# Deformable convolution on one core: spread matmuls of three groups interleaved part by part, and a chunk's twelfth group run with the next chunk's first two

## The chip, the core and the metric

The kernel runs on one core of a Trainium2 chip. The metric is device microseconds of one whole execution. TensorE is called PE here, VectorE DVE, ScalarE ACT, GpSimd POOL and SyncE SP. What an engine's own instruction reader does (register steps, branches, waits of their own) is listed in the profile under the engine's name with a q, as PEq or PEldq.

## What is computed

The input is 8 images of 32 channels, 64x64 pixels. It is normalised per channel and image, passes four blocks and one final deformable convolution, and is added to the raw input:

```python
def _block(x, dc_w, dc_b, of_w, of_b, dw, db):
    h = jax.nn.relu(_deconv2d(x, dc_w, dc_b))          # 3x3, 32 -> 32 channels
    offset = _conv2d(h, of_w, of_b, PAD)               # 3x3, 32 -> 18: (dy, dx) of 9 taps
    return jax.nn.relu(_deform_conv2d(h, offset, dw, db))
...
sampled = bilinear samples of x at (row + tap + dy, column + tap + dx), zero outside
out = einsum('bckhw,ock->bohw', sampled, w) + b
...
x_cat = concatenate(x, in_module)                      # 64 channels
offset = _conv2d(x_cat, fin_off_w, fin_off_b, PAD)
return _deform_conv2d(x_cat, offset, fin_dcn_w, fin_dcn_b)
```

## The kernel before

The images go in two sets of four. A step is one layer for one set, so there are ten: eight of the four blocks, two of the final layer. A step begins with 3x3 convolutions on PE (line 515), then picks by the range of the offsets how wide a window of pixels the samples can come from. In this data the eight block steps take `kind` 0 (window 11x11, 121 positions) and the two final steps `kind` 1 (16x16, in two tiles of 128).

The sampling takes nearly all of a step. The image plane is cut into 32 chunks (16 bands of four rows, two halves). A bilinear weight is a product of a hat function in y and one in x, and the hats are made once for a chunk: ACT takes the distance (`DIST`, line 735), DVE clamps it (line 922), POOL casts it to fp16 and makes the rest as a second fp16 part (`HL`, lines 1103 and 1105, semaphore `hats_full`). The hats sit on four blocks of 32 partitions, one for each image. A *group* is three taps of one image; a chunk has twelve (a kind 1 chunk has two batches of twelve), and group g lies on the 32 partitions of image g mod 4. For a group:

- PE spreads the y hats over the window's positions with a 0/1 table `SEL`: two matmuls, one for each part of `HL` (line 544), into one of three y slots of PSUM; the second raises `y_full`. In this text they are the first and second part of y.
- ACT copies that slot to SBUF (`YC`, line 768), which raises `y_ready`.
- PE spreads the x hats the same way, into one of four x slots (two matmuls, or four for the two tiles of kind 1; `x_full`).
- DVE multiplies the two (`A`, line 917, `product_done`).

A y spread waits until the copy three groups earlier is done, an x spread until the product four groups earlier is done. Both waits are written with a register value, so PE's reader does a register step ahead of each group.

When a chunk's twelve products are there, PE samples: matmuls of `A` with the window's pixels `VT` (line 562) in three parts, each of which ACT copies out of the one PSUM bank `PS` (`SMP`, line 745). Then comes the sum over taps and channels (`deform`, line 575), which ACT takes out (`TMP`, line 728) and DVE adds to the image (line 911). A part of the chunk before runs after groups 4, 7 and 10 of the present one (`sh.after`), the sum of an earlier chunk after group 1 (`sum_after`; in kind 1 only in the second batch).

All of this is one order written out by hand for each engine; semaphores alone tie them together. The chunk loop is unrolled by two: chunks 0 and 1, a hardware loop over pairs, chunks 30 and 31. So every second chunk border is a loop's branch (line 297), the other runs straight through. On ACT the order at a border is: third part's `SMP`, `YC` of group 11, `DIST` of the chunk after the one that begins, `YC` of groups 0 and 1, `TMP`. PE waits at the head of a chunk's body for the chunk's hats (line 630, which the trace shows as line 253), and POOL's order has nothing but the hats.

In kind 0 PE issues y and x of one group, then y and x of the next (lines 613 to 615). In kind 1 it issues the y spreads of a run of groups and then their x spreads (lines 616 to 621); the runs are groups 0-1, 2-4, 5-7, 8-10 and 11.

Of the kernel before, what the change touches and what calls it, by code (L numbers as in the profile page):

```python
# [22 lines left out]
BLK = 4  # L23
COLS = 32
CPX = BLK * COLS
BANDS = SIDE // BLK
CHUNKS = 2 * BANDS
# [73 lines left out]


# [7 lines left out]
def build(nc, t):  # L110

    ctx = ExitStack()
    with ctx:
# [388 lines left out]
        def _(pe):  # L502
# [31 lines left out]
            def spread(sh, g, b, par, table, out, column=0):  # L534

                third, i = divmod(g, IMG)
                q = slice(CH * i, CH * (i + 1))
                for part in range(2):
                    hats = HL[q, part, par, 3 * CPX * third:3 * CPX * (third + 1)]
                    dst = P[0:sh.npos, out, column:column + sh.size]  # L540
                    if sh.kind == 1:
                        hats = hats.rearrange("p (k r c) -> p k r c", r=BLK, c=COLS)[:, :, :, 16 * b:16 * b + 16]
                        dst = dst.rearrange("p (k r c) -> p k r c", r=BLK, c=16)
                    mm = nc.tensor.matmul(dst, SEL[q, table, 0:sh.npos], hats, start=part == 0, stop=part == 1)  # L544
                return mm
# [33 lines left out]
            def body_of(sh):  # L579
# [19 lines left out]
                def batch(c, b, half, prev, before):  # L599
                    def spread_y(g):  # L600

                        pe.wait_ge(y_ready, (c * sh.batches + b) * sh.ngr + g + 1)
                        spread(sh, g, b, half, y_table, g % Y_SLOTS).then_inc(y_full, 1)

                    def spread_x(g):

                        pe.wait_ge(product_done, (c * sh.batches + b) * sh.ngr + g + 1)
                        for tile, table in enumerate(x_tables):
                            mm = spread(sh, g, b, half, table, Y_SLOTS + g % X_SLOTS, sh.size * tile)
                        mm.then_inc(x_full, 1)  # L610

                    for g in range(sh.ngr):
                        if sh.kind == 0:
                            spread_y(g)
                            spread_x(g)
                        elif g in sh.runs:

                            for each in sh.runs[g]:
                                spread_y(each)
                            for each in sh.runs[g]:  # L620
                                spread_x(each)
# [597 lines left out]
```

## Time and profile before

| | |
|---|---|
| time, median of 3 runs | 4313.63 us (4312.2 to 4316.89) |
| the profiled execution: span | 4314.1 us (the page gives no other time of it) |
| PE busy, weight loads | 3880.1 us (90%), 2973.5 us (69%) |
| DVE busy | 2952.5 us (68%) |
| ACT busy | 2786.4 us (65%) |
| POOL busy | 1140.5 us (26%) |
| spread matmuls, line 544 | 21504, 1745.6 us busy |
| copies of y, line 768 | 4608, 1733.9 us busy |
| products, line 917 | 4608, 2311.4 us busy |

The time of the profiled execution lies within the three timed runs, 0.5 us above their median, and nothing is shown outside its span. Busy time of PE is the union of matmuls that overlap: a matmul that is listed with 0.32 us can run beside others. A row of the timeline merges instructions of one kind that follow each other; its first two numbers are the start and the length in us.

### The profile page before, as it was taken

The page shows a single profiled execution, that of the slowest core. Times are in us where ns is not written, and L with a number is a line of the kernel's source. Part 1 is how long each engine was busy: PE and PEld are TensorE (multiplying, and loading weights), DVE is VectorE, ACT ScalarE, POOL GpSimd, SP SyncE. Part 2 cuts the span into 40 slices and gives each one's busy share as a digit, 9 for nine tenths or more (in the row PEclk, how much of TensorE's full clock was granted, in tenths as well). Part 3 has the DMA queues.
Part 4 walks back from the last instruction along what each step waited for, and adds up shares of the span by engine and source line. Part 5 has one row for each costly group of instructions (what it writes and reads, how often), then busy time and mean ns, then how long its engine had stood idle before and what let it go on. Part 6 is the DMA issues. An engine that isn't in the chain of part 4 may idle for free.

```text
span 4314.1 us, 221726 instructions
## 1 busy us (share of the span) xinstructions
PE 3880.1 (90%) x81908; PEld 2973.5 (69%) x81908; DVE 2952.5 (68%) x5858; ACT 2786.4 (65%) x6651; POOL 1140.5 (26%) x645
## 2 busy tenths in 40 slices
PE   4998799699789879979988997998799999799998
PEld 3776577477567657756765775776577777577776
DVE  5885687488567668847856884784577774577775
ACT  2885588388478658837865883885355554255554
POOL 0441243134033214403322431331111110111111
PEclk8999899799989989989998997999799999899999
DMA  4442544344244334424424443443766664666664
GB/s 125 127 127 66 143 125 110 89 126 127 75 132 126 90 106 127 125 76 131 126 71 127 127 114 92 126 125 109 179 154 152 150 150 127 147 154 152 152 150 110
DMA packets 244838, 533.50 MB, mean 124 GB/s; under 512 B 61200, under 2 KB 151824, under 8 KB 227216
## 3 DMA queue, kind: packets, MB, share of 16 engines
q1 hardware_dynamic: 194224, 498.67, 45.0%
q10 hardware_dynamic: 50240, 29.89, 2.4%
q8 instruction: 229, 3.75, 0.4%
q14 instruction: 145, 1.19, 0.1%
HBM read 471.87 MB, written 56.45 MB: 122 GB/s over the span
## 4 chain that ended last, share of the span: by engine, by line
PE 68%; SPq 18%; issue 7%; ACT 2%; DMA 2%; DVE 2%; POOLq 0%; ACTq 0%; DVEq 0%; POOL 0%; PEld 0%; PEldq 0%
PE P L544 26%; PE PS L562 24%; SPq L380 9%; PE P L515 8%; PE PS L575 8%; SPq L388 8%; SPq L370 1%; PE PS L515 1%; ACT H L848 1%; DMA X<-x_dram 1%; PE P L530 1%; DVE FOFF L1032 1%; DMA VT<-ht_store 0%; DVE A L917 0%; DVE ST L1036 0%
## 5 line engine op out<-in xcount | busy, mean ns | idle before, releaser
L917 DVE TENSOR_TENSOR A<-P,YC 121x384 f32<-121x384 f32 (+1 forms) x4608 | 2311.4, 550 | 850.1 <-ACT YC L768 684.5
L544 PE MATMUL P<-HL,SEL 32*121 32x384 f16 (+1 forms) x21504 | 1745.6, 304 | 131.6 <-issue 95.3
L768 ACT ACTIVATE YC<-P 121x384 f32<-121x384 f32 (+1 forms) x4608 | 1733.9, 444 | 98.7 <-PE P L544 65.8
L544 PEld LDWEIGHTS P<-HL,SEL 32*121 32x121 f16 (+1 forms) x21504 | 1126.9, 117 | 513.9 <-issue 228.6
L562 PE MATMUL PS<-A,VT 121*32 121x80 f32 (+1 forms) x40960 | 1342.7, 250 | 51.7 <-DMA VT<-ht_store 15.5
L562 PEld LDWEIGHTS PS<-A,VT 121*32 121x32 f32 (+1 forms) x40960 | 1093.0, 117 | 354.6 <-issue 200.4
L1103 POOL CAST HL<-DIST 128x1152 f16<-128x1152 f32 x320 | 366.3, 1145 | 3066.1 <-DVE DIST L922 3043.8
L745 ACT ACTIVATE SMP<-PS 128x480 f32<-128x480 f32 (+3 forms) x1152 | 593.9, 516 | 638.2 <-PE PS L562 632.9
L1105 POOL TENSOR_TENSOR HL<-DIST,HL 128x1152 f16<-128x1152 f32 x320 | 769.6, 2405 | 58.5 <-POOL HL L1103 58.5
L735 ACT ACTIVATE DIST<-HB,CONST 128x1152 f32<-128x1152 f32 x320 | 400.8, 1252 | 231.4 <-DMA HB<-off_store 128.8
L575 PE MATMUL PS<-SMP,CW 128*64 128x128 f32 x7424 | 476.0, 277 | 5.4 <-ACT SMP L745 5.4
L575 PEld LDWEIGHTS PS<-SMP,CW 128*64 128x64 f32 x7424 | 398.7, 137 | 86.8 <-issue 76.6
L515 PE MATMUL P<-X,W 32*32 32x512 f32 x5040 | 210.0, 664 | 90.7 <-POOLq L256 58.6
L922 DVE TENSOR_SCALAR DIST<-DIST 128x1152 f32<-128x1152 f32 x320 | 240.2, 751 | 10.2 <-ACT DIST L735 10.2
L911 DVE SCALAR_TENSOR_TENSOR X<-X,CONST,TMP 128x128 f32 (+1 forms) x320 | 172.5, 539 | 79.7 <-ACT TMP L728 79.7
L515 PEld LDWEIGHTS P<-X,W 32*32 32x32 f32 x5040 | 128.4, 108 | 141.5 <-issue 114.6
L728 ACT ACTIVATE TMP<-PS,BIAS 128x128 f32<-128x128 f32 x320 | 119.0, 372 | 151.5 <-PE PS L575 151.5
L848 ACT ACTIVATE H<-P,BIAS 32x512 f32<-32x512 f32 x128 | 87.9, 687 | 193.6 <-PE P L515 161.6
L515 PE MATMUL P<-H,W 32*32 32x512 f32 x5040 | 209.5, 637 | 2.7 <-issue 2.7
L1032 DVE SCALAR_TENSOR_TENSOR FOFF<-P,PXB 128x512 f32<-128x512 f32 x70 | 47.9, 684 | 198.5 <-PE PS L515 122.3
L515 PEld LDWEIGHTS P<-H,W 32*32 32x32 f32 x5040 | 138.4, 105 | 62.6 <-issue 29.5
L1016 DVE TENSOR_SCALAR H<-P,BIAS 32x512 f32<-32x512 f32 x96 | 72.0, 750 | 145.8 <-PE P L515 118.3
(61 smaller groups left out, 703.4 us busy)
## 6 DMA issues: line engine op xcount, KB each, us to landing
HB<-off_store SPq DMA_DIRECT2D x2560, 72.0 KB
VT<-ht_store SPq DMA_DIRECT2D x256, 512.0 KB
VT<-ht_store SPq DMA_DIRECT2D x768, 132.0 KB
VT<-ht_store SPq DMA_DIRECT2D x256, 88.0 KB
off_store<-FOFF SPq DMA_DIRECT2D x160, 128.0 KB, 2.6
H<-x_dram SPq DMA_DIRECT2D x5, 2048.0 KB, 14.6
ht_store<-A ACTq DMA_DIRECT2D x32, 256.0 KB, 3.3
ht_store<-VT ACTq DMA_DIRECT2D x32, 256.0 KB, 3.9
```

Of the source, the lines that this page charges most:

```text
L380: sp.dma_start(HB[q:q + AXIS, half, :], src).then_inc(hb_full[half], 16)
L388: sp.dma_start(VT[first:first + sh.win * columns, buf, tile * size:(tile + 1) * size], src).then_inc(vt_full[buf], 16)
L515: mm = nc.tensor.matmul(bank(bank0 + i)[CH * j:CH * (j + 1), :], weights[q, CH * k:CH * (k + 1)], view(row + k // 3 - 1, col + k % 3 - 1)[ ...
L544: mm = nc.tensor.matmul(dst, SEL[q, table, 0:sh.npos], hats, start=part == 0, stop=part == 1)
L562: mm = nc.tensor.matmul(PS[q:q + wide, sh.unit * v:sh.unit * (v + 1)].rearrange("p (k y x) -> p k y x", k=sh.taps, y=BLK), vt[:, img, :], ...
L575: mm = nc.tensor.matmul(PS[64 * pair:64 * (pair + 1), 0:CPX], CW[:, 64 * k:64 * (k + 1)], rhs, start=k == 0, stop=k == sh.taps - 1)
L735: nc.scalar.activation(DIST[:, :], HB[:, half, :], ACT.Abs, bias=HAT_BIAS).then_inc(abs_done, 1)
L745: nc.scalar.activation(smp_px(0, sh, b * sh.blocks + w, s, count), PS[:, 0:sh.unit * count], ACT.Copy).then_inc(ps_free, 1)
L768: nc.scalar.activation(YC[0:sh.npos, g % X_SLOTS, 0:sh.size], P[0:sh.npos, g % Y_SLOTS, 0:sh.size], ACT.Copy).then_inc(y_ready, 1)
L917: return nc.vector.tensor_tensor(dst, x, y, ALU.mult)
L1103: nc.gpsimd.tensor_copy(HL[:, 0, half, :], DIST[:, :]).then_inc(hat_step, 1)
L1105: nc.gpsimd.tensor_tensor(HL[:, 1, half, :], DIST[:, :], HL[:, 0, half, :], ALU.subtract).then_inc(hats_full, 1)
```

## The change

PE's order of spread matmuls is written anew; no other engine's code is touched. A run takes up to three groups, of either kind: the first parts of their y, the second parts, then the first parts of their x, the second parts (in kind 1 for one tile and then the other). Where no sample part stands after group 11, which is so in both kinds here, group 11 (`carries`) is left out of its own chunk or batch and put in front of the next one's run of groups 0 and 1. At a chunk border that place is behind the loop's branch and behind the wait for the new chunk's hats. After the last chunk, group 11 runs alone.

```diff
+        self.carries = int(self.ngr - 1 not in self.after)
...
-            def spread(sh, g, b, par, table, out, column=0):
+            def spread_part(sh, g, b, par, table, out, column, part):
...
+                return nc.tensor.matmul(dst, SEL[q, table, 0:sh.npos], hats, start=part == 0, stop=part == 1)
...
-                    for g in range(sh.ngr):
-                        if sh.kind == 0:
-                            spread_y(g)
-                            spread_x(g)
-                        elif g in sh.runs:
-
-                            for each in sh.runs[g]:
-                                spread_y(each)
-                            for each in sh.runs[g]:
-                                spread_x(each)
+                def run(members):
+
+                    if len(members) > Y_SLOTS:
+                        run(members[:Y_SLOTS])
+                        members = members[Y_SLOTS:]
+                    for n, g, b, half in members:
+                        pe.wait_ge(y_ready, n + 1)
+                        spread_part(sh, g, b, half, y_table, g % Y_SLOTS, 0, 0)
+                    for n, g, b, half in members:
+                        spread_part(sh, g, b, half, y_table, g % Y_SLOTS, 0, 1).then_inc(y_full, 1)
+                    for tile, table in enumerate(x_tables):
+                        for part in range(2):
+                            for n, g, b, half in members:
+                                if tile == 0 and part == 0:
+                                    pe.wait_ge(product_done, n + 1)
+                                mm = spread_part(sh, g, b, half, table, Y_SLOTS + g % X_SLOTS, sh.size * tile, part)
+                                if tile == len(x_tables) - 1 and part == 1:
+                                    mm.then_inc(x_full, 1)
+
+                def batch(c, b, half, prev, before, carried):
+                    first = (c * sh.batches + b) * sh.ngr
+                    for g in range(sh.ngr - sh.carries):
+                        if g in sh.runs:
+                            members = [(first + each, each, b, half) for each in sh.runs[g]]
+                            if sh.runs[g][0] == 0 and sh.carries and carried is not None:
+                                members.insert(0, (first - 1, sh.ngr - 1, *carried))
+                            run(members)
...
                 def tail():
+                    if sh.carries:
+                        run([(CHUNKS * sh.batches * sh.ngr - 1, sh.ngr - 1, sh.batches - 1, 1)])
```

PE at the border in the middle of a loop's pair of chunks, kind 0: before, the third part (line 562) is followed by group 11's four spreads, and only then by the wait for the hats and group 0.

```order
L562 MATMUL PS<-A,VT 32x80 x15
L602 REGISTER_ALU
L544 MATMUL P<-HL,SEL 121x384 [waits y_ready]
L544 MATMUL P<-HL,SEL 121x384
L544 MATMUL P<-HL,SEL 121x384 [waits product_done]
L544 MATMUL P<-HL,SEL 121x384
L252 REGISTER_ALU
L602 ISA [waits hats_full]
L544 MATMUL P<-HL,SEL 121x384 [waits y_ready]
L544 MATMUL P<-HL,SEL 121x384
```

The same place in the change, whose lines 545, 567 and 610 are the old 544, 562 and 602: group 11's first spread is the first one below the wait for the hats.

```order
L567 MATMUL PS<-A,VT 32x80 x15
L254 REGISTER_ALU
L610 REGISTER_ALU [waits hats_full]
L545 MATMUL P<-HL,SEL 121x384 [waits y_ready]
L610 REGISTER_ALU
L545 MATMUL P<-HL,SEL 121x384 [waits y_ready]
L610 REGISTER_ALU
L545 MATMUL P<-HL,SEL 121x384 [waits y_ready]
L545 MATMUL P<-HL,SEL 121x384 x3
L545 MATMUL P<-HL,SEL 121x384 [waits product_done] x3
L545 MATMUL P<-HL,SEL 121x384 x3
```

Group 11 moved behind the wait, and the second part of its y moved behind two more register steps and the first parts of groups 0 and 1.

PE at the end of the loop's body, kind 0: before, group 11 stands between the third part and the branch.

```order
L562 MATMUL PS<-A,VT 32x80 x15
L602 REGISTER_ALU
L544 MATMUL P<-HL,SEL 121x384 [waits y_ready]
L544 MATMUL P<-HL,SEL 121x384
L544 MATMUL P<-HL,SEL 121x384 [waits product_done]
L544 MATMUL P<-HL,SEL 121x384
L297 REGISTER_ALU
L297 COMPARE_AND_BRANCH
```

In the change the branch follows the third part at once, and group 11 is found at the head of the loop's body.

```order
L545 MATMUL P<-HL,SEL 121x384 x3
L596 REGISTER_ALU [waits product_done]
L567 MATMUL PS<-A,VT 32x80 [waits ps_free]
L567 MATMUL PS<-A,VT 32x80 x15
L299 REGISTER_ALU
L299 COMPARE_AND_BRANCH
```

PE between the two batches of a kind 1 chunk: before, all six spreads of group 11 stand ahead of groups 0 and 1 (the sum, line 596, follows).

```order
L562 MATMUL PS<-A,VT 64x144 x7
L602 REGISTER_ALU
L544 MATMUL P<-HL,SEL 128x192 [waits y_ready]
L544 MATMUL P<-HL,SEL 128x192
L544 MATMUL P<-HL,SEL 128x192 [waits product_done]
L544 MATMUL P<-HL,SEL 128x192 x3
L602 ISA
L544 MATMUL P<-HL,SEL 128x192 [waits y_ready]
L544 MATMUL P<-HL,SEL 128x192
L602 REGISTER_ALU
```

In the change the three groups go in step.

```order
L567 MATMUL PS<-A,VT 64x144 x7
L610 ISA
L545 MATMUL P<-HL,SEL 128x192 [waits y_ready]
L610 REGISTER_ALU
L545 MATMUL P<-HL,SEL 128x192 [waits y_ready]
L610 REGISTER_ALU
L545 MATMUL P<-HL,SEL 128x192 [waits y_ready]
L545 MATMUL P<-HL,SEL 128x192 x3
L545 MATMUL P<-HL,SEL 128x192 [waits product_done] x3
L545 MATMUL P<-HL,SEL 128x192 x9
```

Here no wait for hats and no branch lies between; group 0 and 1 moved up beside group 11.

## Rows read from the trace of the kernel before

**Rows 1.** The page, chain that ended last, by line

```profile
PE P L544 26%; PE PS L562 24%; SPq L380 9%; PE P L515 8%; PE PS L575 8%; SPq L388 8%; SPq L370 1%; PE PS L515 1%; ACT H L848 1%; DMA X<-x_dram 1%; PE P L530 1%; DVE FOFF L1032 1%; DMA VT<-ht_store 0%; DVE A L917 0%; DVE ST L1036 0%
```

**Rows 2.** Timeline of ACT over two chunks of the first step (start, us, instructions)

```profile
207.48 1.26 ACT L735 ACTIVATE DIST<-HB,CONST 128x1152 f32<-128x1152 f32 x1
208.64 0.85 ACT L768 ACTIVATE YC<-P 121x384 f32<-121x384 f32 x2
...
213.48 0.57 ACT L745 ACTIVATE SMP<-PS 128x480 f32<-128x480 f32 x1 [0.31 <-PE PS L562]
213.95 1.25 ACT L768 ACTIVATE YC<-P 121x384 f32<-121x384 f32 x3
215.13 0.44 ACT L745 ACTIVATE SMP<-PS 128x320 f32<-128x320 f32 x1
215.56 0.49 ACT L768 ACTIVATE YC<-P 121x384 f32<-121x384 f32 x1
215.95 1.25 ACT L735 ACTIVATE DIST<-HB,CONST 128x1152 f32<-128x1152 f32 x1
```

**Rows 3.** Groups by line and shape: kind 0 copies of y (busy, mean, idle before)

```profile
L768 ACT ACTIVATE YC<-P 121x384 f32<-121x384 f32 x3072 | 1319.9, 500 | 18.7 <-PE P L544 17.0
```

**Rows 4.** Timeline of DVE, same chunk

```profile
209.24 1.02 DVE L917 TENSOR_TENSOR A<-P,YC 121x384 f32<-121x384 f32 x2 [1.31 <-ACT YC L768]
210.18 0.75 DVE L922 TENSOR_SCALAR DIST<-DIST 128x1152 f32<-128x1152 f32 x1
...
212.31 1.94 DVE L917 TENSOR_TENSOR A<-P,YC 121x384 f32<-121x384 f32 x4
```

**Rows 5.** Busy time of DVE from its first product of that chunk (window, us, busy, clock)

```profile
209.24:214.25 5.01, 5.01 (x10) 1.00 0.36 103
```

**Rows 6.** Timeline of PE, same chunk

```profile
211.30 1.14 PE L544 MATMUL P<-HL,SEL 32*121 32x384 f16 x12
...
213.35 1.02 PE L544 MATMUL P<-HL,SEL 32*121 32x384 f16 x12
214.30 0.76 PE L562 MATMUL PS<-A,VT 121*32 121x80 f32 x32
```

**Rows 7.** Timeline of POOL, same chunk

```profile
212.42 2.41 POOL L1105 TENSOR_TENSOR HL<-DIST,HL 128x1152 f16<-128x1152 f32 x1 [0.18 <-POOL HL L1103]
```

**Rows 8.** Single steps of PE's reader, each asked for alone (length ns, start)

```profile
L602 PEldq ALU_OP  x1: 32/32/32, 205.8 to 205.8; - x1
L297 PEldq ALU_OP  x1: 32/32/32, 205.9 to 205.9; - x1
...
L253 PEldq EVENT_SEMAPHORE  x1: 51/51/51, 214.9 to 214.9; - x1
L602 PEldq FUSED_REGOPS  x1: 37/37/37, 215.0 to 215.0; - x1
L602 PEldq ALU_OP  x1: 32/32/32, 215.1 to 215.1; - x1
```

**Rows 9.** Timeline of PE at 206.28, 206.66, 206.667 and 215.125 alone: spreads in flight

```profile
206.28 0.37 PE L544 MATMUL P<-HL,SEL 32*121 32x384 f16 x1
206.49 0.48 PE L544 MATMUL P<-HL,SEL 32*121 32x384 f16 x2
206.49 0.54 PE L544 MATMUL P<-HL,SEL 32*121 32x384 f16 x3
214.99 0.48 PE L544 MATMUL P<-HL,SEL 32*121 32x384 f16 x2
```

**Rows 10.** Timeline of PE in a kind 1 chunk

```profile
3208.71 0.87 PE L544 MATMUL P<-HL,SEL 32*128 32x192 f16 x18
...
3213.95 0.70 PE L544 MATMUL P<-HL,SEL 32*128 32x192 f16 x18
```

**Rows 11.** Timeline of ACT at the starts of steps one and two

```profile
110.54 1.26 ACT L735 ACTIVATE DIST<-HB,CONST 128x1152 f32<-128x1152 f32 x1 [0.29 <-POOL HL L1105]
...
496.08 1.25 ACT L735 ACTIVATE DIST<-HB,CONST 128x1152 f32<-128x1152 f32 x1 [3.76 <-DMA HB<-off_store]
```

More of the change, by code:

```diff
@@ L532, in transposes, with spread @@
                     mm.then_inc(ht_full, 1)
-            def spread(sh, g, b, par, table, out, column=0):
+            def spread_part(sh, g, b, par, table, out, column, part):
                 third, i = divmod(g, IMG)
                 q = slice(CH * i, CH * (i + 1))
-                for part in range(2):
[L539 to L544, printed above, removed]
+                hats = HL[q, part, par, 3 * CPX * third:3 * CPX * (third + 1)]
+                dst = P[0:sh.npos, out, column:column + sh.size]
+                if sh.kind == 1:
+                    hats = hats.rearrange("p (k r c) -> p k r c", r=BLK, c=COLS)[:, :, :, 16 * b:16 * b + 16]
+                    dst = dst.rearrange("p (k r c) -> p k r c", r=BLK, c=16)
+                return nc.tensor.matmul(dst, SEL[q, table, 0:sh.npos], hats, start=part == 0, stop=part == 1)
+            def spread(sh, g, b, par, table, out, column=0):
+                for part in range(2):
+                    mm = spread_part(sh, g, b, par, table, out, column, part)
                 return mm
@@ L597, in sums @@
                     deform(sh, 0).then_inc(ps_full, 1)
[L599 to L610, printed above, removed]
-                    for g in range(sh.ngr):
-                        if sh.kind == 0:
-                            spread_y(g)
-                            spread_x(g)
-                        elif g in sh.runs:
-                            for each in sh.runs[g]:
-                                spread_y(each)
-                            for each in sh.runs[g]:
-                                spread_x(each)
+                def run(members):
[15 more added lines that the diff above has]
+                                    mm.then_inc(x_full, 1)
@@ L633, in body @@
                             prev = (c, band, b - 1, half)
+                            carried = (b - 1, half)
                         elif before == 0:
-                            prev = None
+                            prev = carried = None
                         else:
                             prev = (c - 1, band + half - 1, sh.batches - 1, 1 - half)
-                        batch(c, b, half, prev, before)
+                            carried = (sh.batches - 1, 1 - half)
+                        batch(c, b, half, prev, before, carried)
                 def tail():
+                    if sh.carries:
+                        run([(CHUNKS * sh.batches * sh.ngr - 1, sh.ngr - 1, sh.batches - 1, 1)])
                     if sh.lag == 2:
```

## The prediction

> **What bounds the kernel now.** I read the chain that ended last first, then the timelines of ACT, DVE, PE and POOL over two chunks of the first step, then the steps of PE's reader at the two chunk borders.
>
> The chain gives PE by far the most, with the spreads first [rows 1]. That does not yet make PE the bound: the chain follows an engine back as long as it is busy. In the eight kind 0 steps I look for the cycle that repeats. From one `DIST` on ACT to the next it is 215.95 - 207.48 = 8.47 us [rows 2]. After `DIST` come the copies of y 0 and 1, at 208.64. 0.60 later DVE begins its products, at 209.24 [rows 4], and then it does not stand still for 5.01 us, ten instructions, up to 214.25 [rows 5]: products 0 and 1, the clamp, products 2 and 3, the residual, products 4 to 7. The last four take 1.94; with 0.55 for one, they follow each other at (1.94 - 0.55) / 3 = 0.46, so product 6 ends at 212.31 + 2 x 0.46 + 0.55 = 213.78. PE's x spread of group 10 must wait for it (four x slots). Its two spreads take 0.21 + 0.32 more (below), which gives 214.31, and the third sample part starts at 214.30 [rows 6]. The run of spreads before it began at 213.35 and lasted 1.02; it was waiting for DVE at its end, not for its own matmuls.
>
> Then the border: third part, `SMP` at 215.13, the copy of y 11 at 215.56, `DIST` at 215.95 [rows 2]. A copy that is ready goes 0.10 before the end of a `SMP` (213.48 + 0.57 - 213.95), which here would be 215.13 + 0.44 - 0.10 = 215.47. It starts at 215.56, because y 11 is full only then: PE's first spread of it starts at 214.99 [rows 9]; at the border before, the first started at 206.28 and lasted 0.37, the second started at 206.49 and the third, 0.32 long, ended at 206.97 [rows 9], so it started at 206.65. The steps are 0.21 and 0.16, a later spread lasts 0.32, and y 11 is full at 214.99 + 0.21 + 0.32 = 215.52. ACT's idle time before copies in kind 0, put down to PE's spreads, is 17.0 us [rows 3], over 8 x 31 borders 0.07 each, which is this wait. So the second part of y 11 is on the cycle, and every delay of it moves the copy, `DIST`, copy 0 and DVE's row of ten. The three runs inside a chunk are not on it as far as their own matmuls go.
>
> **What the change does, part by part.**
>
> Runs inside a chunk, kind 0. Interleaving can at most take away the time by which one group starts after another. Run 8-10 must end with x 10, which is let go by product 6, and run 5-7 with x 7, which product 3 lets go in the same way; with the two parts of x one behind the other on the same partitions, their ends stay. In run 2-4, y 4 waits for copy 1 (one of the pair at 208.64, done 209.49), and four spreads follow it on its own partitions in either order. I take 0 for all three. What is worse there: y 2's second part now stands behind y 4's first, so copy 2 comes some 0.3 us later. DVE's clamp (210.18, 0.75 long) covers it, since product 2 starts only after it [rows 4, 5]; uncovered it would cost 0.3 x 248 = 74 us.
>
> The border inside a pair, kind 0. The wait for the hats now stands ahead of y 11. POOL ends the hats at 212.42 + 2.41 = 214.83 [rows 7]; the wait passes at 214.88, the register step follows at 215.03 [rows 8] (asked for in windows of 0.02 us, so good to 0.01), and group 0's first spread, 0.37 long like every first one, ends at 214.99 + 0.48 = 215.47 [rows 9], so it began at 215.10, 0.07 after its register step. In the change y 11 has that place: 215.10 instead of 214.99. The next register step comes 0.05 later (215.15 [rows 8]) and its spread 0.07 after that, so group 0 starts at 215.22, group 1 at 215.34, and the second part of y 11 behind it at 215.36. Its weights are not loaded ahead, so I give it 0.37 like a first one: full at 215.73 instead of 215.52. Cost: 0.21. POOL's hats hang on the clamp, which hangs on copies 0 and 1, so they move with the cycle and give nothing back.
>
> The border with a branch, kind 0. Here the hats come early enough and PE's own reader sets the time: the register step of group 11 is at 205.77, that of the branch at 205.94 [rows 8], y 11's first spread at 206.28 and its second at 206.49, group 0's first at 206.67 (at 206.667 a third one is in flight, ending at 207.03 [rows 9]). In the change the branch's steps come 0.17 sooner, less about 0.04 for the four second parts that now stand behind group 10's wait; y 11 gets group 0's place, 206.67 - 0.13 = 206.54. Groups 0 and 1 follow at 0.12 each, the second part of y 11 starts at 206.79 and is full at 207.16 instead of 206.81. Cost: 0.35.
>
> The sum in kind 0: of 31 borders in a step one is the first (below), 14 have the loop's entry or branch, 16 have none. 16 x 0.21 + 14 x 0.35 = 8.3; 8 steps: 66 us. The first border: before, y 11 is long done when the hats of chunk 1 let `DIST` go at 110.54 [rows 11]; now y 11 and its copy come between: 0.27 from the hats to its first spread and 0.24 for groups 0 and 1 as above, 0.37 to 0.5 for its second part, 0.39 from copy to `DIST` as in [rows 2], less some 0.2 that `DIST` needs after the hats anyway: an estimate of 1.2. In the four steps of the second set ACT waits 3.76 for the hats' input early on [rows 11], which hides that one and about two more borders. 4 x 1.2 - 4 x 0.6 = +2. I take 68 for kind 0.
>
> How far the two border prices may go: down to what the third y slot demands anyway (y 1 cannot start before copy 10 is done, one of three from 213.95 on, 1.25 long: 215.20, so y 11's second part about 215.26 + 0.37 = 215.63, cost 0.1, 248 x 0.1 = 25 us), if the reader gets its steps done ahead. Up, the branch's could be 0.45 if it also waits for the hats as the other does: 14 x 8 x 0.1 = 11 more.
>
> Kind 1. The run 11, 0, 1 ahead of the sum lasts 0.87, a run of three that starts together 0.70 [rows 10]: 0.17 a chunk, once in two batches (the other border waits for copy 11 and product 0, as before). 2 x 32 x 0.17 = 11 us gained; PE is the bound in those steps as long as no copy or product is late; where one is, the 0.17 is hidden. Between 0 and 11. At the border with the hats PE's third part covers the reader's steps (its matmuls are fewer and longer than kind 0's); without that cover it costs 31 x 2 x 0.3 = 19.
>
> Sum: 4314.1 + 68 - 11 = 4371 us, against the profiled execution's span, which is 0.5 above the median of the runs; nothing is added for that.
>
> One rule of the Trainium skill speaks for a gain instead. At 215.125 the second spread in flight is group 0's first, 0.08 before the second part of y 11 starts, which stands ahead of it in the program [rows 9]. "TensorE: Matmul & The Clock Gate", section "The mechanism", says matmuls start and end in program order and only weight loads are pulled ahead. By that a run of group after group would need 3 x 0.53 + 0.32 = 1.9 us and an interleaved one 0.9; the rows show 1.02 and 1.14 for the former [rows 6], so the measurement decides.
>
> **The rivals.**
>
> (a) PE is the bound after all and the interleaved runs are shorter. A run in step would be four spreads on the same partitions, 0.21 + 2 x 0.16 + 0.37 = 0.90, against 1.14 and 1.02 [rows 6]: 0.24 + 0.12 a chunk, 248 x 0.36 = 89 us, and with kind 1 4314 - 89 - 11 = 4214. For it: the chain. Against: DVE's 5.01 of 5.01 [rows 5]. It decides once x 7 and x 10 no longer wait for DVE. The rule above would have it so, and by more.
>
> (b) The small delay: PE's reader runs far enough ahead, and only copy 10 holds y 1 and so y 11. 25 - 11: 4328. For it: the reader was half a microsecond ahead of y 11 at the branch (205.77 for 206.28). Against: the wait for the hats passed only 0.05 after POOL was done.
>
> (c) Nothing net: the copy of y 11 gets the delay, but the third sample part comes earlier by as much. 4314, within 9. Against: x 10 still waits for product 6.
>
> (d) The order inside runs 2-4 costs too: DVE's clamp does not cover copy 2 everywhere. 68 + 37 (half of 74) - 11: 4408.
>
> **How the numbers follow.** Forecast 0.72, at 4371 with its own range 4345 to 4390; (a) 0.07, (b) 0.10, (c) 0.04, (d) 0.07. The range from 4328 to 4395 holds the forecast and (b)'s upper half and leaves out (a), (c) and (d). What a measurement can tell from no change is 0.2%, 9 us: faster 0.07, same 0.05, slower 0.88.
>
> **What would show it.** In the profile after: the distance of two `DIST` in a kind 0 step, 8.47 inside a pair, goes to about 8.68, and at a branch it grows by 0.35. The copy of y 11 starts more than 0.6 after its `SMP` begins, not 0.43. ACT's idle time before copies of y, put down to PE, rises from 17 us to 80. Runs 5-7 and 8-10 keep their 1.0 to 1.1, or PE waits after them. DVE's row of ten still takes 5.0. Kind 1 chunks shorten by 0.17. It would be wrong if the product row on DVE opened gaps (then (d)), or if sample parts moved forward against copy 0 (then (a)).

## The result, and the profile after

After the change the kernel takes 4359.85 us (median of 4, 4356.87 to 4361.24), before 4312.91 (4310.68 to 4316.89): a ratio of 1.0107, 95% interval 1.0094 to 1.012. It is slower by 47 us; 58 were forecast. The profiled execution after has a span of 4359.5, at a mean granted clock of 0.939 (0.940 before).

ACT's timeline at a border inside a pair (the columns as in [rows 2]):

```profile
218.51 1.25 ACT L781 ACTIVATE YC<-P 121x384 f32<-121x384 f32 x3
219.69 0.44 ACT L758 ACTIVATE SMP<-PS 128x320 f32<-128x320 f32 x1
220.32 0.49 ACT L781 ACTIVATE YC<-P 121x384 f32<-121x384 f32 x1 [0.19 <-PE P L545]
220.71 1.25 ACT L748 ACTIVATE DIST<-HB,CONST 128x1152 f32<-128x1152 f32 x1
```

The copy of y 11 starts 0.63 after its `SMP`; it was 0.43 [rows 2]. Everything after it follows at the old distances. What it waits for stands on POOL and in PE's weight loads at the same border:

```profile
216.99 2.41 POOL L1118 TENSOR_TENSOR HL<-DIST,HL 128x1152 f16<-128x1152 f32 x1 [0.18 <-POOL HL L1116]
```

```profile
219.67 0.74 PEld L545 LDWEIGHTS P<-HL,SEL 32*121 32x121 f16 x12 [0.24 <-ACT YC L781]
```

The hats end at 216.99 + 2.41 = 219.40, and the first weights, those of y 11, are loaded 0.27 later: 0.05 + 0.15 + 0.07, as read from [rows 7, 8, 9]. The releaser shown, a copy, is not the last thing waited for: the copy that frees y 11's slot, copy 8, is the first of the three from 218.51 and over by 219.01, so the hats are. y 11's second part is the fourth matmul of this stretch; the first four, asked for alone:

```profile
219.68 0.60 PE L545 MATMUL P<-HL,SEL 32*121 32x384 f16 x4
```

In the single records the fourth starts 0.23 after the first (0.26 was forecast) and lasts 0.37 as forecast, up to 220.28; the copy starts 0.04 later.

At a branch border the copy waits longer, and `DIST` comes 0.63 after the copy instead of 0.39, since ACT's own loop branch lies between them (so it did before):

```profile
210.66 0.44 ACT L758 ACTIVATE SMP<-PS 128x320 f32<-128x320 f32 x1
211.41 0.49 ACT L781 ACTIVATE YC<-P 121x384 f32<-121x384 f32 x1 [0.32 <-PE P L545]
212.04 1.26 ACT L748 ACTIVATE DIST<-HB,CONST 128x1152 f32<-128x1152 f32 x1
```

```profile
207.95 2.41 POOL L1118 TENSOR_TENSOR HL<-DIST,HL 128x1152 f16<-128x1152 f32 x1 [0.18 <-POOL HL L1116]
```

The hats end at 210.36 there; in the single records PE's branch ends at 210.43 and its wait for the hats passes at 210.48, so it is PE's reader that sets the time.

Two groups by line and shape, the first to be read beside [rows 3], the second (ACT's readings of the first two sample parts) beside the same group before, under them:

```profile
L781 ACT ACTIVATE YC<-P 121x384 f32<-121x384 f32 x3072 | 1311.7, 495 | 135.3 <-PE P L545 132.5
L758 ACT ACTIVATE SMP<-PS 128x480 f32<-128x480 f32 x512 | 292.5, 571 | 177.2 <-PE PS L567 175.5 <-issue 0.2
```

```profile
L745 ACT ACTIVATE SMP<-PS 128x480 f32<-128x480 f32 x512 | 292.5, 571 | 271.6 <-PE PS L562 266.3 <-issue 1.2
```

The idle time before copies rose by 117 us, but the readings of the sample parts lost 94. Copy 2 now waits 0.21 in each chunk, and the reading of the first part behind it waits 0.21 instead of 0.55 (means over kind 0). Idle time that only moves along an engine's row costs nothing; what y 11 adds is what counts.

In kind 1 the run ahead of the sum now lasts 0.67 where [rows 10] had 0.87:

```profile
3245.42 0.67 PE L545 MATMUL P<-HL,SEL 32*128 32x192 f16 x18
3246.02 2.19 PE L580 MATMUL PS<-SMP,CW 128*64 128x128 f32 x36
```

To see where the 45.3 us between the spans went, I take from both traces the starts of ACT's copies, twelve to a chunk in kind 0 and twenty-four in kind 1: the distance of two copies 0 across each kind of border (for each step the median over its pairs, or over the loop's thirteen branches; then the mean over the steps), and the time from a step's first copy to its last. The columns of us stand for one profiled execution of each kernel, the median for the timed runs; the two values at the branch are for the steps of the first set and of the second. In the unrolled kernel only every second border of the branch column is still a branch.

| kernel | median us | inside pair | branch | eight kind 0 steps | two kind 1 steps |
|---|---|---|---|---|---|
| before | 4312.9 | 8.45 | 8.72, 8.80 | 2233.2 | 1154.4 |
| after | 4359.9 | 8.66 | 9.04, 9.05 | 2286.2 | 1144.5 |
| no carry | 4316.1 | 8.45 | 8.72, 8.84 | 2230.5 | 1154.8 |
| carry, old order | 4337.1 | 8.57 | 8.92, 8.96 | 2265.2 | 1144.4 |
| carry in kind 1 | 4300.8 | 8.45 | 8.72, 8.78 | 2232.0 | 1143.4 |
| y 11 early | 4300.9 | 8.45 | 8.71, 8.76 | 2232.7 | 1142.9 |
| after, clamp earlier | 4330.1 | 8.56 | 8.84, 8.91 | 2259.0 | 1142.7 |
| after, y 11 first | 4334.7 | 8.57 | 8.93, 8.97 | 2262.4 | 1143.3 |
| both of these | 4294.1 | 8.29 | 8.77, 8.88 | 2223.1 | 1144.0 |
| kind 1, clamp earlier | 4292.0 | 8.29 | 8.58, 8.96 | 2220.6 | 1141.1 |
| kind 1, residual later | 4290.0 | 8.29 | 8.59, 8.98 | 2221.0 | 1143.7 |
| kind 1, both | 4294.2 | 8.29 | 8.61, 8.94 | 2220.9 | 1144.5 |
| kind 1, clamp first | 4296.1 | 8.34 | 8.61, 8.94 | 2222.7 | 1142.5 |
| kind 1, clamp earlier, unrolled | 4464.2 | 8.31 | 8.61, 8.92 | 2226.3 | 1302.7 |

After less before: +53.0 in kind 0, -9.9 in kind 1, +2.1 between and ahead of the steps: 45.2 of 45.3.

### The profile page after: what moved, and what is told of

Its sections match the earlier page's. It is cut to its first block, busy times and chain, and to the rows that moved or that the text cites. A ratio compares the mean times of both kernels' runs of the same rounds, so it can differ in the third digit from the quotient of the medians.

```text
span 4359.5 us, 221726 instructions
## 1 busy us (share of the span) xinstructions
PE 3836.1 (88%) x81908; PEld 2720.9 (62%) x81908; DVE 2958.7 (68%) x5858; ACT 2792.9 (64%) x6651; POOL 1140.7 (26%) x645
## 4 chain that ended last, share of the span: by engine, by line
PE 70%; issue 10%; ACT 8%; SPq 6%; DVE 3%; DMA 2%; ACTq 1%; DVEq 0%; POOLq 0%; PEld 0%; PEldq 0%
PE P L545 28%; PE PS L567 26%; PE P L517 8%; ACT YC L781 6%; PE PS L580 5%; SPq L382 3%; DVE A L930 1%; SPq L390 1%; SPq L372 1%; PE PS L517 1%; ACT H L861 1%; DMA X<-x_dram 1%; PE P L532 1%; DVE FOFF L1045 1%; DVE ST L1049 0%
## 5 line engine op out<-in xcount | busy, mean ns | idle before, releaser
L545 PE MATMUL P<-HL,SEL 32*121 32x384 f16 (+1 forms) x21504 | 1689.2, 308 | 231.5 <-issue 100.7
L781 ACT ACTIVATE YC<-P 121x384 f32<-121x384 f32 (+1 forms) x4608 | 1712.5, 442 | 228.6 <-PE P L545 205.2
L545 PEld LDWEIGHTS P<-HL,SEL 32*121 32x121 f16 (+1 forms) x21504 | 875.5, 116 | 823.4 <-ACT YC L781 292.8
```

The source lines that it names most:

```text
L545: return nc.tensor.matmul(dst, SEL[q, table, 0:sh.npos], hats, start=part == 0, stop=part == 1)
L781: nc.scalar.activation(YC[0:sh.npos, g % X_SLOTS, 0:sh.size], P[0:sh.npos, g % Y_SLOTS, 0:sh.size], ACT.Copy).then_inc(y_ready, 1)
```

## The experiments

Each ratio below is to the kernel before, timed again beside that run (medians of 4311.0 to 4314.5).

### Is it the carried group at all?

Group 11 in its own chunk, the part by part order kept:

```diff
-        self.carries = int(self.ngr - 1 not in self.after)
+        self.carries = 0
```

> Group 11 stays in its own chunk, in a run of its own, in all ten steps; the part by part order of every other run is the changed kernel's. Theory (border): the price of the change is only that group 11's y spread stands behind the hats wait or the loop branch and behind two more register steps. Kind 0's chunk period goes back to 8.45 us inside a pair and 8.72 at the branch (from 8.66 and 9.04), the first period of a step from 8.9-9.1 to 7.7-7.9, and kind 1 loses its gain (17.54 back to 17.73 a chunk). Time 4313, between 4309 and 4318. Rival (order): the order inside the runs 2-4, 5-7 and 8-10 costs by itself; then kind 0 stays above 8.6 and the time above 4340. Rival (TensorE bound): fewer idle columns in the runs help kind 0 on their own; then the time falls below 4305.

4316.05 us, 1.0012 (1.0004 to 1.0021), in the range expected and 5 us above the kernel before, of which the bodies in the table show nothing. Kind 0 is back at 8.45 and 8.72, and kind 1 has lost its whole gain. The new order inside the runs changes neither kind by more than 3 us: rivals (a) and (d) of the prediction fall. Copy 2 waits here too (76.8 us of idle time before copies put down to PE), and it costs nothing. One part of the expectation failed: a step's first period is 8.38, not 7.7 to 7.9. It is 7.8 and 7.6 before, in the two sets, so the new order lengthens it by itself: in a step's first chunk, where no sample part lies between the runs, ACT now waits 0.67 ahead of each run of three copies, where the waits before were some 0.2. One row of the kernel without the carry, under it one of before:

```profile
107.74 1.25 ACT L781 ACTIVATE YC<-P 121x384 f32<-121x384 f32 x3 [0.67 <-PE P L545]
```

```profile
105.92 1.46 ACT L768 ACTIVATE YC<-P 121x384 f32<-121x384 f32 x3 [0.19 <-PE P L544]
```

### The carry in the old order

Group 11 carried, but inside a run group by group as before:

```diff
-                    for n, g, b, half in members:
-                        pe.wait_ge(y_ready, n + 1)
-                        spread_part(sh, g, b, half, y_table, g % Y_SLOTS, 0, 0)
...
+                    if sh.kind == 0:
+                        for member in members:
+                            spread_y(*member)
+                            spread_x(*member)
+                    else:
...
```

> Group 11 is carried into the next chunk's first run as in the changed kernel, but every run goes group by group as before (y and x in kind 0, all y and then all x in kind 1). Theory (border): of the 0.20 us inside a pair some 0.08 were the two register steps and first parts of groups 0 and 1 that stand between group 11's two y parts; here 0.12 stays inside a pair and 0.22-0.26 at the branch, so kind 0 pays some 35 of the 53 us, and kind 1, which now has neither the overlap of the parts nor group 11 alone, keeps some 5 of its 10. Time 4345, between 4335 and 4355. Rival (order alone): nothing is paid at the border, time 4305 to 4315. Rival (wait alone): the whole price is the hats wait and the branch, time 4360 or above.

4337.08 us, 1.0059 (1.0047 to 1.0071). Inside a pair 8.57, which is the 0.12 expected, and at the branch 0.20 in the first set and 0.16 in the second, a little less than expected. Kind 1 keeps its whole 10 us where half was expected; hence 4337 and not 4345. Its gain is group 11 no longer being alone in a run, not the parts.

### The carry in kind 1 alone

```diff
-        self.carries = int(self.ngr - 1 not in self.after)
+        self.carries = int(kind == 1)
```

> Group 11 is carried in the two kind 1 steps alone; the eight kind 0 steps keep it in its own chunk, with the part by part order in their runs. Theory (border): kind 0 as before the change (8.45 and 8.72), kind 1 17.54 a chunk: 4303, between 4299 and 4308, the only part of the change that gains. Rival (order): kind 0 above 8.6, time above 4335. Rival (kind 1's gain is the order, not the carried group): same time as the kernel without any carry.

4300.83 us, 0.9978 (0.9967 to 0.9988), as expected: the gaining part of the change, by itself.

### y 11 ahead of the wait

In kind 0 the y spread of group 11 whole at the end of its own chunk, x 11 carried:

```diff
+                    late = [m for m in members if sh.kind == 1 or m[1] < sh.ngr - 1]
...
                         if b == sh.batches - 1 and g == sh.sum_after and before >= sh.lag:
                             sums(c - sh.lag)
+                    if sh.kind == 0:
+                        pe.wait_ge(y_ready, first + sh.ngr)
+                        spread(sh, sh.ngr - 1, b, half, y_table, (sh.ngr - 1) % Y_SLOTS).then_inc(y_full, 1)
```

> As the changed kernel, but in kind 0 group 11's y spread stays whole at the end of its own chunk, ahead of the hats wait and the branch; only its x spread is carried into the next run. Theory (border): the chain to the next DIST needs y 11 and not x 11, whose product 11 has time until copy 0 is read; kind 0 goes back to 8.45 and 8.72, and the time is 4303, between 4298 and 4310. Rival (x 11 as well): product 11 heads DVE's row without gaps; if x 11 arrives after DVE is free, each chunk is longer by that time, 0.1 to 0.4 us, and the time is 4325 to 4400.

4300.92 us, 0.9974 (0.9965 to 0.9984), as expected. ACT at a border inside a pair:

```profile
216.64 0.44 ACT L762 ACTIVATE SMP<-PS 128x320 f32<-128x320 f32 x1
217.07 0.49 ACT L785 ACTIVATE YC<-P 121x384 f32<-121x384 f32 x1
217.46 1.25 ACT L752 ACTIVATE DIST<-HB,CONST 128x1152 f32<-128x1152 f32 x1
```

The copy comes 0.43 after its `SMP` again. x 11 may be late; y 11 may not. That puts the 53 us of kind 0 on one spread, that of y 11; its two parts were moved together, so this run doesn't tell them apart.

### Is it the hats?

The changed kernel, with DVE's clamp in kind 0 after product 0, so that POOL gets its input one product earlier:

```diff
-                            if b == 0 and g == sh.next_at + 1 and not last:
+                            if b == 0 and g == sh.next_at + sh.kind and not last:
```

> The changed kernel, with one thing moved on DVE in kind 0: the clamp of the next chunk's distances runs after product 0 instead of after product 1, so that POOL's hats end some 0.45 us earlier against copy 0. Theory (the hats wait is what holds the carried group 11): in the profile after, TensorE's reader passes the hats wait 0.04 us after the hats end and reaches group 11's second y part 0.52 us later; with the hats 0.45 us earlier the reader does its steps while the third sample part still runs, and the border price inside a pair falls from 0.20 us to 0.00-0.08, at the branch from 0.32 to 0.00-0.15. Kind 0 loses 10 us instead of 53: time 4313, between 4303 and 4328. Rival (register steps): the price is the steps and the lost order themselves, whenever the hats come; then time 4350 to 4360. Rival (copy 1 or 4 held by the later product 1): chunks grow, time above 4365.

4330.09 us, 1.0036 (1.0023 to 1.0049): between the theory and the rival, so the expectation failed. The period inside a pair fell by 0.10, not by 0.20. PE's weight loads and ACT at that border:

```profile
216.92 0.17 PEld L545 LDWEIGHTS P<-HL,SEL 32*121 32x121 f16 x2
217.34 0.51 PEld L545 LDWEIGHTS P<-HL,SEL 32*121 32x121 f16 x10 [0.25 <-ACT YC L781]
```

```profile
216.04 1.25 ACT L781 ACTIVATE YC<-P 121x384 f32<-121x384 f32 x3
217.15 0.47 ACT L758 ACTIVATE SMP<-PS 128x320 f32<-128x320 f32 x1
217.76 0.49 ACT L781 ACTIVATE YC<-P 121x384 f32<-121x384 f32 x1
```

y 11 and group 0 now start early, at 216.92. Then PE stands, because group 1's first part needs the y slot that copy 10 frees: 216.04 + 1.25 = 217.29, and the loads go on 0.05 later. Only then comes y 11's second part. This is the limit that the prediction named for its rival (b), and it stands right behind the hats. The clamp moved something else as well, which the next run shows.

### The same move without the carry

```diff
-        self.carries = int(self.ngr - 1 not in self.after)
+        self.carries = int(kind == 1)
...
-                            if b == 0 and g == sh.next_at + 1 and not last:
+                            if b == 0 and g == sh.next_at + sh.kind and not last:
```

> The same move of the clamp where group 11 is carried in kind 1 alone. Theory: in kind 0 nothing waits for the hats here, DVE's row from product 0 to product 7 holds the same instructions, so the chunk stays 8.45 and 8.73 us: 4301, between 4294 and 4306. Rival (product 1 0.67 us later holds the spreads and copies behind it): chunks grow by up to 0.3 us, time up to 4375. Rival (copy 1 had been awaited in the row): row up to 0.1 us shorter, time down to 4276.

4292.01 us, 0.9951 (0.9939 to 0.9964): not unchanged as expected, but 9 us below the kernel with the carry in kind 1 alone; inside a pair 8.29 instead of 8.45. The rival that copy 1 had been awaited is not the reason, since product 2 starts 2.20 after copy 0 in both. On DVE the residual became shorter, and so everything behind it earlier:

```profile
209.68 0.34 DVE L924 SCALAR_TENSOR_TENSOR X<-X,CONST,TMP 128x128 f32 x1
209.94 1.95 DVE L930 TENSOR_TENSOR A<-P,YC 121x384 f32<-121x384 f32 x4
```

```profile
208.53 1.15 POOL L1116 CAST HL<-DIST 128x1152 f16<-128x1152 f32 x1 [4.80 <-DVE DIST L935]
```

POOL's cast ends at 209.68, when the residual starts. In the kernel with the carry in kind 1 and the old place of the clamp the residual starts while the cast runs and is late:

```profile
211.41 0.61 DVE L924 SCALAR_TENSOR_TENSOR X<-X,CONST,TMP 128x128 f32 x1
```

```profile
210.73 1.14 POOL L1116 CAST HL<-DIST 128x1152 f16<-128x1152 f32 x1 [4.97 <-DVE DIST L935]
```

It ends at 212.02, 0.15 after the cast's 211.87. So against a kernel with the clamp here, the carry in the experiment before costs 8.56 - 8.29 = 0.27 inside a pair. PE's stand there is put down to copy 10; that all of the 0.27 hangs on y 11's place in the run is shown by the run with both away, below.

### The residual later

The carry in kind 1 alone, the residual behind product 8:

```diff
+        self.carries = int(kind == 1)
...
-                            if before >= sh.lag and b == sh.batches - 1 and g == sh.sum_after + 2:
+                            if before >= sh.lag and b == sh.batches - 1 and g == sh.sum_after + (2 if sh.kind else 7):
```

> Group 11 carried in kind 1 alone, and on DVE in kind 0 the residual of two chunks ago runs after product 8 instead of after product 3. Theory (the chunk's cycle runs DIST, copies 0 and 1, DVE's row without gaps up to product 6, x 10, third sample part, its reading, y 11's copy, DIST): the residual's 0.53 us leave the row ahead of product 6; the period falls until the next limit, which is ACT's 0.7 us of idle time per chunk or TensorE's, both small, so 0.2 us of 0.53 are expected: 248 chunks by 0.2 give 4250, between 4190 and 4290. Rival (DVE's row is not on the cycle; TensorE or ACT sets it): 4301, between 4294 and 4306.

4289.95 us, 0.9948 (0.9935 to 0.9961): above the expected 4250 and at the upper end of its range. The direction is right, DVE's row up to product 6 is on the cycle, but it stops at 8.29. There ACT has no idle time from copy 8 on: against copy 0, product 6 comes 0.34 earlier, the third `SMP` only 0.07.

### y 11 first in the run

The changed kernel, y 11's two parts ahead of the others:

```diff
                         pe.wait_ge(y_ready, n + 1)
-                        spread_part(sh, g, b, half, y_table, g % Y_SLOTS, 0, 0)
+                        if g == sh.ngr - 1:
+                            spread(sh, g, b, half, y_table, g % Y_SLOTS).then_inc(y_full, 1)
+                        else:
+                            spread_part(sh, g, b, half, y_table, g % Y_SLOTS, 0, 0)
...
+                        if g < sh.ngr - 1:
+                            spread_part(sh, g, b, half, y_table, g % Y_SLOTS, 0, 1).then_inc(y_full, 1)
```

> The changed kernel, but in the carried run group 11's two y parts go first, ahead of the register steps and first parts of groups 0 and 1; all the rest, the part by part order too, is as changed. Theory (border): inside a pair 0.12 instead of 0.20, at the branch 0.20 instead of 0.30, as in the kernel that carried group 11 in the old order; kind 1 keeps its 10 us. Time 4337, between 4331 and 4343: what is left is the hats wait and the branch. Rival (what parted the two kernels is the order of the x parts): 4355 to 4360.

4334.65 us, 1.0053 (1.004 to 1.0066), as expected. The two register steps and first parts of groups 0 and 1 are worth 0.08 inside a pair (8.66 to 8.57) and 0.11 at the branch of the first set (9.04 to 8.93); what comes ahead of them 0.12 and 0.21.

### Both away

The last edit and the clamp after product 0 together, everything carried:

```diff
+                        if g == sh.ngr - 1:
+                            spread(sh, g, b, half, y_table, g % Y_SLOTS).then_inc(y_full, 1)
...
+                            if b == 0 and g == sh.next_at + sh.kind and not last:
```

> The changed kernel with both of these: the clamp after product 0 (hats 0.46 us earlier) and group 11's two y parts ahead of the first parts of groups 0 and 1. With the clamp alone the two y parts lay 0.43 us apart, because group 1's first part between them waited for copy 10 to free its place (copy 10 ended 6.56 us after copy 0, the part started at 6.61). Theory (the border's price is the hats wait, then copy 10, each of them by way of the order in the run): with both gone the carried group costs nothing in kind 0; the period is that of the kernel with the clamp moved and no carry in kind 0, 8.29 inside a pair and 8.75 at the branch; time 4292, between 4286 and 4302. Rival (the loop branch and the added wait cost by themselves): inside a pair 8.41 and at the branch 8.95, time 4320 to 4330.

4294.11 us, 0.9961 (0.9947 to 0.9974): 8.29 inside a pair, and kind 0 as a whole within 3 us of the kernel with the clamp there that carries nothing in kind 0.

```profile
216.48 0.47 ACT L762 ACTIVATE SMP<-PS 128x320 f32<-128x320 f32 x1
216.82 0.51 ACT L785 ACTIVATE YC<-P 121x384 f32<-121x384 f32 x1
217.21 1.25 ACT L752 ACTIVATE DIST<-HB,CONST 128x1152 f32<-128x1152 f32 x1
```

The copy starts 0.34 after `SMP`, without idle time. The price of the carried group is the hats wait, and behind it copy 10 by way of the order in the run; inside a pair nothing is left when both are gone. At the branch of the first set 0.19 stays (8.77 against 8.58): there PE's own branch and wait lie ahead of y 11, and no run takes these away.

### In search of a better kernel

Both moves on DVE together, the carry in kind 1 alone:

```diff
+        self.carries = int(kind == 1)
...
+                            if b == 0 and g == sh.next_at + sh.kind and not last:
...
+                            if before >= sh.lag and b == sh.batches - 1 and g == sh.sum_after + (2 if sh.kind else 7):
```

> Both moves on DVE together: the clamp after product 0 and the residual after product 8, group 11 carried in kind 1 alone. Theory (each of them alone had taken away the same thing: the residual's 0.27 us longer stay, 0.61 instead of 0.34 us, while POOL copies the hats; what is left at 8.293 us is ACT without idle time from copy 8 on and the sample parts before it): they don't add, 8.29 and 8.75, time 4291, between 4284 and 4296. Rival (DVE's row sets the period in all three): product 6 comes another 0.3 us earlier and the period falls with it, time 4215 to 4260.

4294.15 us, 0.9954 (0.9941 to 0.9968): they don't add, as expected.

The clamp ahead of product 0, the residual after product 8, the carry in kind 1 alone:

```diff
+        self.carries = int(kind == 1)
...
+                            if sh.kind == 0 and g == 0 and not last:
+                                clamp(c + 1)
                             if g == 0 and before > 0:
...
+                            if before >= sh.lag and b == sh.batches - 1 and g == sh.sum_after + (2 if sh.kind else 7):
```

> Group 11 carried in kind 1 alone; on DVE in kind 0 the clamp runs ahead of product 0, in the time that DVE waits there, and the residual after product 8, when POOL is done with the hats. In the two runs that moved one of them the period inside a pair was 8.293 us and ACT had no idle time left from copy 8 to DIST, but 0.21, 0.31 and 0.21 us ahead of copy 2's run, the second and the first reading of the sums. Theory (these readings wait for product 3 and product 0): product 3 comes some 0.25 us earlier and product 0 0.22 us later, so the second reading moves up and the first back; of 0.7 us of ACT's idle time 0.15 are expected to go: 248 chunks by 0.15 give 4255, between 4235 and 4290. Rival (product 0 holds group 4's x spread and the first sample part, and nothing makes it up): period up to 0.22 us longer, time up to 4345. Rival (TensorE sets 8.29): 4290.

4296.08 us, 0.9959 (0.9945 to 0.9973): product 0 comes 0.20 later, the first reading 0.18 later and the second 0.10 earlier; the period is 8.34. It misses its range.

The loop over bands unrolled once, with the clamp after product 0 and the carry in kind 1:

```diff
-            with eng.Fori(0, BANDS - 2) as pair:
-                body(2 * pair + 2, pair + 1, 0, 2, False)
-                body(2 * pair + 3, pair + 1, 1, 2, False)
+            with eng.Fori(0, (BANDS - 2) // 2) as two:
+                for u in range(2):
+                    body(4 * two + 2 * u + 2, 2 * two + u + 1, 0, 2, False)
+                    body(4 * two + 2 * u + 3, 2 * two + u + 1, 1, 2, False)
```

> The kernel with group 11 carried in kind 1 alone and the clamp after product 0, with the loop over bands unrolled once: four chunks per pass instead of two, so 8 instead of 15 branch borders a step. Theory (a branch border costs each chunk that holds one 0.45 us: 8.75 against 8.29 us): 7 borders less in 8 kind 0 steps give 25 us, and kind 1, whose two chunk periods weren't told apart, 0 to 6: time 4265, between 4257 and 4280. Rival (the 0.45 us is not the branch but what differs between an even and an odd chunk): unchanged, 4287 to 4297. Rival (a longer loop is fetched more slowly): above 4297.

4464.15 us, 1.0346 (1.0332 to 1.036): the third case, and by far more than it said. Kind 0 gained nothing (2226.3 against 2220.6); kind 1 lost 160 us. In kind 1 PE stands once in each pass, some 5 us in one step and 9 in the other, for nothing that the profile names; in the first of the two:

```profile
3237.99 1.20 PE L568 MATMUL PS<-A,VT 128*64 128x144 f32 x16
3244.62 1.37 PE L546 MATMUL P<-HL,SEL 32*128 32x192 f16 x19 [5.43 <-issue]
```

The page of this kernel, instruction queues (packets, MB, share), and under it that of the kernel that isn't unrolled:

```profile
q8 instruction: 415, 6.80, 0.7%
q14 instruction: 273, 2.24, 0.2%
```

```profile
q8 instruction: 227, 3.72, 0.4%
q14 instruction: 145, 1.19, 0.1%
```

The program's text is fetched nearly twice as much, and the trace's DMA records tell when. On q8 each of kind 1's seven unrolled passes brings 10 to 13 packets of 16 KB, so these passes are read anew each time; in kind 0 the first pass brings 6 and the later ones none, or one at the end. Not unrolled, kind 1's passes bring none after the second. A pass of kind 1 is longer by 10 us in one step and 15 in the other, of which PE's one stand is 5 and 9; the rest is not told apart. q14 too brings 4 to 10 packets of 8 KB in each of those passes; whose they are and what they cost stays open.

The lowest medians of all are those of the two kernels with the carry in kind 1 and either move on DVE, 4290 and 4292 us, below both kernels of this case. From the three at 4294 to 4296 they are not told apart: the intervals of their ratios overlap.

## Why the prediction was right, and where its sizes were off

- **The cycle and the place.** The cycle by `DIST`, copies, DVE's row and y 11 held: moving y 11 alone ahead of the wait gives all of kind 0 back, and shortening DVE's row shortens the chunk. The row itself kept its length: product 7 starts 5.06 after copy 0 in both kernels.
- **Border inside a pair, 0.21.** Measured 0.20, split as the steps had it. That the hats "move with the cycle and give nothing back" was right: by the records of POOL and ACT inside a pair they end 6.20 us after copy 0 in both kernels (medians). The floor that the prediction named for rival (b), copy 10, is not what y 11 waits for in the changed kernel, where the hats and the register steps behind them come later; it is once the hats come earlier, and the expectation of that run, which failed, had left it out.
- **Border with a branch, 0.35.** That PE's reader and not the hats sets the time there was right; the size was off: 0.32 in the first set and 0.25 in the second. 16 x 0.20 + 14 x 0.32 = 7.7 and 16 x 0.20 + 14 x 0.25 = 6.7 a step; four steps of each give 58 us instead of 66.
- **First border and absorbed borders, +2.** Mis-sized: the bodies show 53, so -5. The first period grows by 1.1 to 1.3, where 1.2 was expected, but that agreement is luck: 0.6 to 0.8 of it stands in the kernel without any carry, from the order of the parts, which the prediction put at nothing, and y 11 behind the hats adds only 0.45 to 0.54. In the first set the next period then gives 0.4 back. The four steps of the second set take only 5.4 us more each, those of the first 7.8. Beside the hats' input, which the prediction named, the second set awaits another: PE's waits for the window's pixels (us, times, longest), before and after:

```profile
PE PS L562 <- DMA VT<-ht_store: 15.5, 29, 1.9
```

```profile
PE PS L567 <- DMA VT<-ht_store: 5.2, 4, 2.2
```

  From chunk 4 to chunk 28, 9.7 us of this lie in the second set before, none in the first, and none in either after. So a chunk that grows hides such a wait there; how many of the borders this accounts for isn't shown.
- **Runs inside a chunk, 0.** Right in a step's later chunks, by the kernel without the carry. The cover named for copy 2 held, but the forecast of 80 us of idle time before copies left copy 2's own wait out: 76.8 us without any carry, 132.5 with it.
- **Kind 1, -11.** -9.9; carried in the old order it is -10 too. A chunk lost 0.20 (17.73 to 17.53, medians), 0.17 were forecast.
- **The sum.** 45 instead of 57: 8 from the borders, 7 from the first and the hidden ones, less 1 in kind 1 and 2 between and ahead of the steps (8 + 7 - 1 - 2 = 12). (a) falls: with the new order and no carry, the chunk of kind 0 stays at 8.45.

## What to carry to other kernels

Before instructions of one stage are moved into a run of the next, look for what stands at the front of that run for another reason: a wait put there for its later members now holds the carried one. If one half of what is carried feeds the cycle (y 11) and the other has slack (x 11), carry the half with slack. And in a run in step, each member's wait stands ahead of every member's second part.

## What the hardware showed unexpectedly

- DVE's residual reads two operands from SBUF. Of its 280 executions of one shape in the changed kernel, 224 begin under POOL's cast, 0.46 us before its end, and take 611 ns on average; the other 56 take 343, as all 280 do with the clamp earlier, where the cast is over or within 0.02 us of its end. The products beside POOL's subtraction take 0.55 in all these kernels.

```profile
L924 DVE SCALAR_TENSOR_TENSOR X<-X,CONST,TMP 128x128 f32 x280 | 156.1, 558 | 0.0
```

```profile
L924 DVE SCALAR_TENSOR_TENSOR X<-X,CONST,TMP 128x128 f32 x280 | 96.1, 343 | 0.0
```

  (The changed kernel, and the one with the carry in kind 1 and the clamp earlier; the mean of 558 mixes the two cases.) The Trainium skill, "SBUF — State Buffer", section "Who interferes with whom", states that a DVE instruction with two SBUF inputs contends with a GpSimd instruction that reads SBUF. The trace agrees, with the residual ending 0.15 after the cast in all 224.
- Unrolling cost 160 us in kind 1 and next to nothing in kind 0. In the trace PE's records of one pass are 1305 in kind 1 and 828 in kind 0, unrolled 2608 and 1649. The Trainium skill, "Runtime: NRT & Kernel Launch", section "Instruction fetch mechanics", gives PE room for 2048 instructions. By that a pass of 2608 would not fit and the other three would, and the trace agrees: of the four, that pass alone is fetched anew each time. That q8 is PE's queue is not shown, but its packets in a loop's first passes go with PE's records: 3 for 828, 6 for 1649, 5 or 6 for 1305. The same section says that a taken branch whose target isn't in the current 2-page window forces a fetch; by that, read for PE, a pass of 1305 would be fetched anew as well, but in the trace it isn't, and the measurement decides.
- With the clamp earlier a branch border takes 8.58 in the first set, 0.29 above one inside a pair, of which ACT's branch shows 0.24 (0.63 and 0.39 above). Unrolled, the borders of the first set that lost their branch take 8.35 (median), so there the branch was the price. In the second set a branch border takes 8.96; there the trace shows PE waiting for the window's pixels (us, times, longest; first not unrolled, then unrolled):

```profile
PE PS L567 <- DMA VT<-ht_store: 32.8, 55, 1.9
```

```profile
PE PS L568 <- DMA VT<-ht_store: 48.2, 78, 1.8
```

  From chunk 4 to chunk 28, 19.2 us of the first row lie in the second set and 5.4 in the first; unrolled 26.2 and 13.4. So kind 0 unrolled lost 7 of 15 branch borders a step and got no shorter while this wait grew by 15 us. Why the pixels come later in the second set stays open.
